# Context attentions of a two-layer transformer on one core: scores computed once, softmax in rows of queries, exponentials turned by TensorE

## The reference, cut to what matters

```python
# layer 0: x1 = x + cross_attention(adaLN(x), adaLN(ctx))
scores = einsum('bqhd,bkhd->bhqk', q, k) / sqrt(dh)     # 16 heads of 32, 512 queries, 77 keys
attn = softmax(scores, axis=-1)
out = einsum('bhqk,bkhd->bqhd', attn, v).reshape(B, Lq, H)
x_q + (out @ Wp + bp)
# layer 1: x2 = x1 + gate * self_attention(modulate(ln(x1)))   (512 keys)
#          x3 = x2 + cross_attention(ln(x2), ln(ctx))           (77 keys, the same form as layer 0)
#          x3 + gate * mlp(modulate(ln(x3)))
```

## Time and profile before

| | |
|---|---|
| median of 3 runs | 2545.93 us (2542.42 to 2553.8) |
| profiled execution | 2551.88 us, of which the span of the trace is 2550.1 us |
| PE busy | 2408.3 us, 94% of the span |
| DVE, ACT, POOL busy | 1390.8, 1025.2 and 582.4 us (55, 40 and 23%) |
| DMA | 354.19 MB, 48.4% of 16 engines for the main queue |
| chain that ended last | 81% PE, 7% DVE, 4% ACT, 3% issue, 3% DMA |

### The profile page before, as it was taken

The page is one execution under the profiler, slowest core; times in us unless marked ns, Lnnn a source line. Parts: engine busy times, 40 slices in busy tenths (PEclk is TensorE's granted clock), DMA queues, the critical chain, the costliest instruction groups (busy, mean ns, idle before and its releaser), DMA issues.

```text
span 2550.1 us, 32330 instructions
## 1 busy us (share of the span) xinstructions
PE 2408.3 (94%) x12048; PEld 1688.5 (66%) x12048; DVE 1390.8 (55%) x2463; ACT 1025.2 (40%) x1831; POOL 582.4 (23%) x325
## 2 busy tenths in 40 slices
PE   6889999999999899999998789999999999999999
PEld 5656666578877344444444457667588888888887
DVE  4566666654456777877777457666643222322221
ACT  3444444433322555555554334444442322233232
POOL 2101211210000466666665412111211011101100
PEclk9889999999999899999999899999999999999999
DMA  6687767555574546565553478787431101110110
GB/s 209 188 208 225 210 188 216 174 168 194 190 239 150 120 114 157 138 149 136 124 148 92 127 184 218 202 222 194 153 108 58 58 1 58 58 51 7 58 42 17
DMA packets 261323, 354.19 MB, mean 139 GB/s; under 512 B 61027, under 2 KB 109243, under 8 KB 261166
## 3 DMA queue, kind: packets, MB, share of 16 engines
q1 hardware_dynamic: 259998, 348.27, 48.4%
q0 software_dynamic: 1168, 3.85, 0.4%
HBM read 233.78 MB, written 116.69 MB: 137 GB/s over the span
## 4 chain that ended last, share of the span: by engine, by line
PE 81%; DVE 7%; ACT 4%; issue 3%; DMA 3%; SPq 1%; POOL 1%; DVEq 0%; ACTq 0%; POOLq 0%
PE banks L396 43%; PE banks L2195 14%; PE banks L1901 6%; PE banks L1923 4%; PE banks L1880 4%; PE banks L1935 2%; PE banks L1318 2%; PE banks L1332 2%; PE banks L1339 2%; PE banks L354 2%; DMA norm_x<-x 1%; ACT wide L377 1%; DVE negated_max L1815 1%; DVE norm_x L321 1%; PE banks L765 1%
## 5 line engine op out<-in xcount | busy, mean ns | idle before, releaser
L1979 ACT ACTIVATE self_exponentials<-banks 128x512 f32<-128x512 f32 x512 | 286.4, 594 | 291.2 <-PE banks L1935 138.7
L1815 DVE TENSOR_REDUCE negated_max<-banks 128x1 f32<-128x512 f32 x512 | 329.9, 677 | 100.4 <-PE banks L1880 98.9
L1781 POOL TENSOR_TENSOR self_exponentials<-self_exponentials,self_exponentials 128x2048 f32<-128x2048 f32 x64 | 294.5, 4602 | 202.5 <-ACT self_exponentials L1979 202.5
L2195 PE MATMUL banks<-mlp_w_down_hi,out_parts 128*128 128x512 f32 x1024 | 333.8, 389 | 0.1
L337 POOL TENSOR_SCALAR norm_rstd<-norm_mean_var 128x4 f32<-128x4 f32 x32 | 8.0, 249 | 1341.3 <-DVE norm_mean_var L316 1341.3
L2152 DVE TENSOR_TENSOR out_parts<-wide,out_parts 128x512 fp32r<-128x512 f32 x128 | 93.0, 727 | 371.2 <-ACT out_parts L2224 371.2
L2214 ACT ACTIVATE wide<-banks,bias_columns 128x512 f32<-128x512 f32 x128 | 88.3, 690 | 426.0 <-PE banks L396 426.0
L1901 PE MATMUL banks<-self_query_stack,self_key_stack 98*128 98x512 f32 x512 | 233.3, 457 | 7.8 <-ACT self_exponentials L1979 4.9
L1901 PEld LDWEIGHTS banks<-self_query_stack,self_key_stack 98*128 98x128 f32 x512 | 97.6, 191 | 185.9 <-ACT self_exponentials L1979 147.3
L2195 PEld LDWEIGHTS banks<-mlp_w_down_hi,out_parts 128*128 128x128 f32 x1024 | 192.2, 188 | 40.5 <-DVE cross_last_x_rows L1261 0.5
L1880 PE MATMUL banks<-self_key_stack,self_query_stack 96*128 96x512 f32 x512 | 208.6, 411 | 6.3 <-DVE negated_max L1815 5.1
(11 more groups left out here) (208 smaller groups left out, 5323.6 us busy)
## 6 DMA issues: line engine op xcount, KB each, us to landing
L_query_stack<-q_parts_L SPq DMA_DIRECT2D x96, 256.0 KB, 4.9
norm_x<-x SPq DMA_DIRECT2D x24, 1024.0 KB, 7.5
self_query_stack<-q_parts_self SPq DMA_DIRECT2D x96, 256.0 KB, 4.1
self_key_stack<-k_parts_self SPq DMA_DIRECT2D x96, 256.0 KB, 6.3
cross_query_stack<-q_parts_cross SPq DMA_DIRECT2D x96, 256.0 KB, 4.9
x_rows<-x SPq DMA_DIRECT2D x23, 1024.0 KB, 5.9
x<-x_rows SPq DMA_DIRECT2D x22, 1024.0 KB, 5.0
q_parts_L<-out_parts SPq DMA_DIRECT2D x32, 512.0 KB, 3.7
```

The costliest lines, as they stand in the source:

```text
L1781: e.tensor_tensor(self.p[kt - 1][:], self.p[kt - 1][:], self.p[kt][:], ALU.add).then_inc(self.paired.sem, 1)
L1815: e.tensor_reduce(k.nm[n % 2][:, h * NT + t:h * NT + t + 1], k.bank[:, self.max_banks.of["max", i], :], AX_X, ALU.max, negate=True).then_i ...
L1979: e.activation(self.p[kt][:, h, :], k.bank[:, self.scores.of["score", i], :], ACT.Exp, scale=SCALE).then_inc(self.exp.sem, 1)
L2195: mm = e.matmul(bank, l, w, start=j == 0 and q == 0, stop=j == JC - 1 and q == 2)
```

## The change

The scores are computed once, and the softmax stays in rows of queries (128 queries on the partitions, four heads of 77 keys in a row of 308). DVE takes the negated maxima (L1185). Then the even tiles go one way and the odd ones another: for an even tile DVE scales the maxima to a bias (L1175) and ACT exponentiates from PSUM, four instructions 128x77 with bias and a running sum (L1352); for an odd tile DVE subtracts the maxima (L1179), ACT exponentiates 128x308 in place (L1347) and DVE sums (L1202). DVE inverts the 16 sums (L1212), POOL multiplies the group's 1,232 exponentials by them (L1135), two groups ahead of their use. PE turns them, 16 transposes a group (L1280), ACT copies the turned tiles out (four 77x512 copies, L1366), PE multiplies by the values (L1294), and ACT and DVE split the heads (L1377, L1221). The stacks of queries and keys, the stores and fetches of queries, the second scores, the products with ones, the rows of maxima and DVE's turning and spreading of sums are gone.

More of the change, by code:

```diff
@@ L903 @@
     split: object = nothing
-    load_keys: object = nothing
     load_diagonals: object = nothing
@@ L1207, in maxima, with heads @@
         def maxima(n):
[L1208 to L1212 removed]
+            negated, exponentials, biases = k.nm[n % 2], self.e[n % self.ES], self.biases[n % 2]
+            for done in (self.freed_negated + self.freed_rows if n < 2 else (self.exp((n - 1) * NT - 1),)):
+                dve.wait_ge(*done)
+            def heads(t):
+                return slice(t * GH, (t + 1) * GH)
@@ new lines, in maxima, with sum_heads @@
+                if t == 1:
+                    for done in (self.freed_e[n] if n < self.ES else (self.flipped((n - self.ES) * GH + GH - 1),)):
+                        dve.wait_ge(*done)
+                    bias(0)
+                elif t == 2:
+                    lower(1)
+                elif t == 3:
+                    bias(2)
+                yield
+            lower(3)
+            sum_heads(n, 1)
+            yield
+        def sum_heads(n, t):
+            i = n * NT + t
+            dve.wait_ge(*self.exp(i))
+            e.tensor_reduce(self.sums[n % 2][:, t * GH:(t + 1) * GH], self.e[n % self.ES][:, t, :].rearrange("p (h k) -> p h k", k=S),
+                            AX_X, ALU.add).then_inc(self.summed.sem, 1)
@@ L1354, in project @@
                 yield
-        return ContextSteps(turn=lambda b: self.norm.tensor(e, pe, b), query=query, maxima=maxima, max_rows=max_rows,
-                            attend=attend, project=project, values=values)
+        return ContextSteps(turn=lambda b: self.norm.tensor(e, pe, b), query=query, maxima=maxima, attend=attend,
+                            project=project, values=values)
     def scalar(self, e, act):
@@ L1421, in finish @@
                     act.wait_ge(*done)
-            e.copy(k.o[n % 6][:, 0, :], k.o_wide[n % 2][:]).then_inc(self.heads_hi.sem, 1)
+            e.activation(self.o[n % 7][:, 0, :], k.bank[:, self.heads.of["heads", n], :], ACT.Copy).then_inc(self.heads_hi.sem, 1)
             yield
-        return ContextSteps(split=lambda p: self.w.split_hi(e, act, p), turn=turn, query=query, max_rows=max_rows,
+            yield
+        return ContextSteps(split=lambda p: self.w.split_hi(e, act, p), turn=turn, query=query, maxima=maxima,
                             attend=attend, finish=finish)
```

312 lines of the change are left out of this document (113 added, 199 removed).

## The result

The change is slower: 2683.94 us median (2681.98 to 2685.86) against 2544.55 us, ratio 1.054 (95% interval 1.0513 to 1.0566); 2544.55 is the median of four runs of the kernel before, of which the table above has three. I had forecast 2609 us and at most 2648. The direction was right, the size was not: +139 us in place of +64.

What follows compares the result with a forecast made beforehand. The prediction took PE's work and one tight passage a batch as the bound: 2551.9 - 26 (PE) + 56 (passage) + 24 (POOL) + 9 (clock) = 2614.9, less 6.0 to the runs' median, 2609 us; range 2515 to 2648.

Steps and rivals of the forecast that it cites:

- What bounds the kernel, and where: Both context stages: PE's own work sets the time, with one tight place a batch, where g = 3 meets g = 0.
- the signs that were named: PE busy down 1.0 to 2.3 us a batch, x_lo waits about 2.5, long biases, cross clock below 1.00, idle 5 to 9.
- PE's work, -26 us: Both stages: 8.0 us a batch removed, 5.7 to 7.0 added; gain 1.65 over 16 batches (-16 to -37).
- 77 columns of weights make a pack cheaper: New transpose packs: if time goes with columns, a pack costs 0.35 us, not 0.44, so 5.7 a batch.
- The passage, +56 us: From g = 3 to g = 0, PE waits grow 4.3 us a batch in cross, 3.7 in L0, seven passages each.
- the query part: In g = 0, PE's wait for the query's low part grows from 0.63 to 1.5 us in both stages.
- POOL beside DVE, +24 us: POOL's multiplication holds DVE's four-column bias, 1.4 and 2.0 us late; full price 48, middle taken (0 to +48).
- Clock, +9 us: In cross, longer waits bring half clock costing 2.5 us a batch, 17 over seven, or nothing; +9 taken.
- Faster by PE's work alone: Rival: waits at the passage do not grow, so only PE's work counts; 2520 or 2509 us, chance 0.25.
- The turning as cause of the clock: Rival: more transposes alone lower cross's clock to 0.95; 2555 us, or 2640 with the main case's waits; chance 0.05.
- No measurable change: Rival: growth at the passage eats PE's gain; 2548 us, in 2533 to 2559, chance 0.12.
- the prediction's own bounds: Whole kernel: the low and high ends of the main case's terms add up to 2537 and 2651 us.

Runs made afterwards that it cites:

- odd_late_packs: all_odd_late with the norm's packs of transposes a step earlier in group g = 3; 2556.19 us, ratio 1.0044.
- double_ones: The kernel before with the product of the exponentials with ones done twice in each group, into the same bank; 2584.49 us, ratio 1.0136.
- early_reciprocal: The change with DVE's reciprocal one step earlier, right behind the last sum, so POOL's multiplication starts a tile earlier; 2617.44 us, ratio 1.0302.
- lower_first: The change with the odd tile's subtraction on DVE moved ahead of x_lo and the residual sum; 2656.05 us, ratio 1.0445.
- before_wait_long: The kernel before, with ACT writing the third x_hi of a norm in 32 pieces in cross from the second batch; 2560.74 us, ratio 1.0063.
- before_turns: The kernel before with 16 more packs of four identity transposes a batch, which nothing reads; 2637.85 us, ratio 1.0374.
- three_orders: The change with the odd tile's subtraction ahead of x_lo, the reciprocal a step earlier and g = 1's score pass a step later; 2595.59 us, ratio 1.0207.
- all_odd_late: The change with every tile treated as odd, last two subtractions and reciprocal earlier, g = 1's score pass a step later; 2553.28 us, ratio 1.0026.
- before_wait: The kernel before, with ACT writing the third x_hi of a norm in ten pieces in cross from the second batch; 2549.85 us, ratio 1.0017.

## Why the prediction was right in direction and wrong in size

1. **What bounds the kernel, and where.** Right. PE's work, and one passage a batch; the change lost its time at that passage. Of the signs that were named, the waits on x_lo, L1352 ahead of L381, biases of 1 us and more, a clock below 1.00 and 5 to 9 us of idle PE came true; PE's busy time a batch did not fall but rose to 50.5 us, as it holds the stretches at half clock.

2. **PE's work, -26 us.** Too large; the runs leave it near nothing. The premise that 77 columns of weights make a pack cheaper fell: at full clock a turned pack holds PE as long (1661.22 to 1661.58) as a norm's pack did, and the matmul behind it starts 0.31 before the next.

```profile
1661.22 0.60 PE L1280 MATMUL banks<-identity,cross_exponentials 128*77 128x128 f32 x4
1661.58 0.48 PE L396 MATMUL banks<-x_hi,cross_w_q_hi 128*128 128x512 f32 x1
1661.89 0.39 PE L396 MATMUL banks<-x_lo,cross_w_q_hi 128*128 128x512 f32 x1
```

   That is the dear end, 16 us. From the periods: 57.6 less 7.1 of waits and 7.6 of clock is 42.9 in cross, 0.6 under the 43.5 of before; in odd_late_packs, at a clock of 1.00, PE's busy time is 173.10 / 4 = 43.3. In L0 the same sum gives no gain. By pieces, the ones cost 0.85 a group in cross (double_ones) and not 0.97, and a pack 0.41: 4 x (0.85 + 0.92 + 0.11) - 16 x 0.41 = 0.9. The gain is 0.2 to 0.9 a batch of cross.

3. **The passage, +56 us.** Right in its steps, somewhat too large in size. early_reciprocal, where hardly a bias is held at the passage, has 0.98 + 2.03 = 3.0 us at the packs in cross where 3.9 were worked out, and 1.2 for the query part where 1.5 were. Over both stages its waits grow by 3.0 and 2.5 us a batch, 7 x 5.5 = 39 us. lower_first and early_reciprocal took away the parts that they should.

4. **POOL beside DVE, +24 us, half of the price.** The full one, 48, was nearer. The four-column bias is held like the 512-column instruction of the earlier trace rows: 0.88 and 1.42 us, and up to 3.1 at the worst. POOL's own takes 2.25, not 2.8, so the bias comes 0.7 and 1.3 late and not 1.4 and 2.0; with the wait for the residual sum, which had not been seen, early_reciprocal took 2.9 + 3.2 us of waits a batch away, 7 x 6.1 = 43 us. With the clock behind them it gained 66. Points 3 and 4 together gave 80, and the waits grew by 7 x (5.9 + 5.7) = 81: that these agree so well is luck, one error up and one down. The Trainium skill, "SBUF — State Buffer", section "Who interferes with whom", says that the operation's mode and the order of issue decide; the trace agrees (0.88 and 1.42 beside L1135, 0.16 elsewhere). I should have followed the nearest row of the same operation.

5. **Clock, +9 us.** This is the step that failed. The prediction took one dip of L0 as the price (2.5 us), once a batch, in cross alone, and at half. Even that dip was read too short: the 5 us of the earlier trace rows lie inside a stretch of 7, which costs 3.4.

```profile
386.00:393.00 7.00, 6.60 (x46) 5.23 (x47) 2.32 (x7) 1.67 (x5) 0.00 (x0) 0.51 1.12 275
```

   Both places of a passage in cross make a dip, of 7 to 10 us, and L0's grow too: 7.6 us a batch in cross and 2.2 more than before in L0, over seven passages 53 + 15 = 68 in place of 9. With the measured terms the sum is 2545.9 - 5 (PE, 0.6 a batch of cross) + 7 x (5.9 + 5.7) + 68 = 2690, against 2684. The clock accounts for 59 us of what the forecast missed, PE's work for 21. before_wait_long shows that a wait alone does this, before_turns and three_orders that the transposes don't.

6. **Rivals.** Faster by PE's work alone: it needed waits that don't grow, and PE's work does not shrink enough for it in any case. The turning as cause of the clock: refuted, and the Trainium skill's rule in "TensorE: Matmul & The Clock Gate", section "Part 4: PE-mode transpose", that transposes do not count as TensorE being busy, made no difference here: the trace has 1.00 with 20 packs a batch in before_turns. No measurable change: the growth was far more than the gain. The range ended at 2648, 3 below the 2651 that the prediction's own bounds add up to; the result is beyond both.

By parts, a batch of cross: -0.6 (PE's work) + 5.9 (waits) + 7.6 (clock) = 12.9, as measured; this is no check of its own, since the -0.6 is what the other two leave of the period. A batch of L0: 5.7 + 2.2 = 7.9, measured 8.2. The first and the last batches have another order and are not taken apart here.

What stays open: how the clock follows from the waits in detail, and whether all_odd_late could go below the kernel before by another order on DVE. In cross a wait of 0.77 us (before_wait) left the clock at 1.00, and so did one of 1.85 in all four batches (three_orders); one of 2.16 was followed by half clock each time. But in L0 of the kernel before 0.75 and 0.92 close together are followed by half clock in each of the three batches, while 0.97 and 0.92 in cross of three_orders are in only one of four; and the same waits have stretches of different length behind them. No kernel here that does the whole work beats the kernel before by more than the measurement can tell.

## What to carry to other kernels

In a kernel that runs TensorE at its full clock, price a new wait of about 2 us or more with the stretch at half clock behind it, at each place where it stands, and look behind shorter waits too: here the clock cost 68 us beside the 81 of the waits, and in cross more than they did. It can work the other way too: in double_ones, added work that covered a wait brought the clock back and nearly paid for itself in L0. Look at a static order for what stands ahead of the instruction that frees a PSUM bank, and let small instructions on VectorE of the kind that a row shows to be held (here TENSOR_SCALAR) start when GpSimd is idle; moving one reciprocal by a step was worth 66 us. A saving in TensorE's work is only a saving when it is measured with its neighbours, and when no other engine's order comes next.

## What the runs showed of the hardware that I had not expected

- A running sum on ACT leaves a second instruction, ACTIVATION_READ_ACCUMULATOR, of 0.20 us after each exponential of 0.33; the starts of such exponentials are 0.30 apart, 1.2 us for four.
- A TENSOR_SCALAR of four columns is held by a GpSimd instruction as one of 512 is (0.16 us alone, 1.42 beside it).
- Work added to PE can cost almost nothing where it covers a wait: L0 at a clock of 1.00 in double_ones, 0.94 in the kernel before.
- The same L0, unchanged, reached its fourth norm at 209.31 us in one profile and at 201.47 us in another, of kernels that differ only in cross.
